# Cross-attention in a decoder kernel: the plain scores of two heads issued ahead of the two turned ones in each step

## The reference: what is computed

```python
# b = 32 slices of 128 rows, 8 heads of 16 rows; q is the normalised x, k and v are the context
qh = q.reshape(b * h, d // h, m)          # (256, 16, 256)
kh = k.reshape(b * h, d // h, -1)
vh = v.reshape(b * h, c // h, -1)
qk = einsum('bdm,bdn->bmn', qh, kh) * scale
sm = softmax(qk, axis=-1)
ret = einsum('bmn,bcn->bcm', sm, vh)
x = x + ret
```

## Time and profile before

| | us |
|---|---|
| median of 3 runs (1822.62 to 1827.89) | 1824.02 |
| the profiled execution | 1821.79 |
| its span, first to last instruction | 1819.6 |
| first to last turned score, bankXT of line 1295 | 946.6 to 1421.8 |

### The profile page before, as it was taken

How to read it: one execution, slowest core, us unless ns; L and a number is a source line. 1 busy time by engine, 2 the same in 40 slices (tenths; PEclk the granted TensorE clock), 3 DMA queues, 4 the chain that set the end, 5 groups by cost and what they waited for, 6 DMA issues and landing times. The chain is left out here.

```text
span 1819.6 us, 45303 instructions
## 1 busy us (share of the span) xinstructions
PE 1723.4 (95%) x15418; PEld 1383.0 (76%) x15419; DVE 1184.2 (65%) x2266; ACT 815.6 (45%) x1577; POOL 835.4 (46%) x1295
## 2 busy tenths in 40 slices
PE   3999999999999999999869999999999899999997
PEld 2888888888888888888757777777777799866664
DVE  5777777777777777776657788888886454422221
ACT  3434334334334334334317777777776543311111
POOL 4455555555555555555434444444443331144443
PEclk9999999999999999999869999999999899999999
DMA  5021121121121121121233444444443256422221
GB/s 187 19 60 40 48 58 38 48 58 37 49 58 36 50 58 37 49 58 39 53 98 96 119 117 117 123 119 123 124 123 97 89 159 236 136 64 68 67 63 40
DMA packets 145103, 148.17 MB, mean 81 GB/s; under 512 B 26114, under 2 KB 139718, under 8 KB 143242
## 3 DMA queue, kind: packets, MB, share of 16 engines
q1 hardware_dynamic: 138218, 120.74, 24.0%
q0 software_dynamic: 5664, 13.93, 2.4%
q10 hardware_dynamic: 1152, 12.58, 2.0%
HBM read 93.20 MB, written 53.98 MB: 81 GB/s over the span
## 5 line engine op out<-in xcount | busy, mean ns | idle before, releaser
L1195 DVE TENSOR_REDUCE xmax<-bankX 128x4 f32<-128x1024 f32 x256 | 308.7, 1217 | 63.5 <-PE bankX L1284 58.8
L1143 ACT ACTIVATE xe<-bankXT 128x512 f32<-128x512 f32 x512 | 292.0, 598 | 93.9 <-PE bankXT L1295 79.5
L1295 PE MATMUL bankXT<-stq,stk 98*128 98x256 f32 x1024 | 230.9, 312 | 11.7 <-ACT xe L1143 5.1
L369 POOL TENSOR_TENSOR roped<-ropeC,ropeD 128x512 f32<-128x512 f32 x160 | 205.2, 1289 | 56.7 <-DVE ropeD L530 56.7
L1295 PEld LDWEIGHTS bankXT<-stq,stk 98*128 98x128 f32 x1024 | 157.6, 193 | 54.7 <-ACT xe L1143 35.7
L557 DVE TENSOR_TENSOR oTl<-bankV,oTh 128x512 fp32r<-128x512 f32 x128 | 88.1, 688 | 166.7 <-ACT oTh L445 166.7
L662 PE MATMUL bankQ<-wqh,xnTh 128*128 128x512 f32 x384 | 188.9, 492 | 0.0
L1284 PE MATMUL bankX<-stk,stq 96*128 96x256 f32 x1024 | 171.1, 291 | 14.5 <-DMA rw<-in_rw 11.0
L361 POOL TENSOR_TENSOR prob<-prob,rden 128x1024 f32<-128x1024 f32 x64 | 121.9, 1904 | 88.8 <-DVE rden L553 88.4
L1284 PEld LDWEIGHTS bankX<-stk,stq 96*128 96x128 f32 x1024 | 145.0, 196 | 18.0 <-DMA rw<-in_rw 11.2
L728 PE MATMUL bankO<-woh,oTh 128*128 128x256 f32 x512 | 152.5, 298 | 0.0
(11 more groups left out here) (189 smaller groups left out, 3907.0 us busy)
## 6 DMA issues: line engine op xcount, KB each, us to landing
stackk_d<-chl SPq DMA_DIRECT2D x96, 128.0 KB, 2.3
stackq_d<-q2hl SPq DMA_DIRECT2D x96, 128.0 KB, 2.3
stk<-stackk_d SPq DMA_DIRECT2D x32, 384.0 KB
stq<-stackq_d SPq DMA_DIRECT2D x128, 96.0 KB
wexp<-in_wexp ACTq DMA_DIRECT2D x8, 1536.0 KB, 7.9
x_d<-x SPq DMA_DIRECT2D x64, 128.0 KB, 1.9
xrden<-inv_d SPq DMA_DIRECT2D x64, 128.0 KB, 2.5
xin<-xg_d SPq DMA_DIRECT2D x39, 128.5 KB, 2.1
```

The lines of the kernel that those rows point to most:

```text
L369: nc.gpsimd.tensor_tensor(roped[c % 3][:], ropeC[c % 2][:], ropeD[c % 2][:], ALU.add).then_inc(s_rsum, 1)
L1143: nc.scalar.activation(xe[q][:].rearrange("p n m -> p (n m)"), bT[:, q % 2, :], ACT.Exp).then_inc(s_xe, 1)
L1195: nc.vector.tensor_reduce(xmax[tile[1] % 2][:, :, a:b + 1:b - a].rearrange("p m h -> p h m"), bS[:, 2 * (pr % 2):2 * (pr % 2) + 2, :].rear ...
L1295: ins = nc.tensor.matmul(bT[:, q % 2, n * D:(n + 1) * D], stk[p][0:98, hd // 4, n * P:(n + 1) * P], stq[p][0:98, hd, :], start=True, stop= ...
```

## The change

In every step of PE's body in the cross-attention the plain scores of two heads are issued first, then the two turned scores. Before, the plain scores stood between the first and the second turned score. What follows at the end of a step (turns, results, logits, rank) keeps its place, and the programs of the other four engines are the same.

```diff
             def body(tile, one, two, three, four, five):
                 w, v, y = prev(tile, 1), prev(tile, 2), prev(tile, 4)
                 for r in range(STEPS):
+                    if one:
+                        scores_x(tile, r)
                     if two and r >= LAG:
                         turned_scores_x(w, 2 * (r - LAG))
                     if three and r < LAG:
                         turned_scores_x(v, 2 * (r + STEPS - LAG))
-                    if one:
-                        scores_x(tile, r)
                     if two and r >= LAG:
                         turned_scores_x(w, 2 * (r - LAG) + 1)
                     if three and r < LAG:
```

## The result

The change makes the kernel slower by 0.77%: the ratio to the kernel before is 1.0077 (95% interval 1.006 to 1.0093). The medians are 1838.6 us (5 runs, 1835.6 to 1844.3) and 1826.8 (5 runs, 1822.6 to 1829.9; three of them are those shown ahead). The forecast was 12 us more and 1836.0 as the time; the ratio says 14.1 more, and the medians are 11.8 apart. The profiled execution took 1838.6, its span 1836.5, which is 16.9 over the span before.

What follows compares the result with a forecast made beforehand. PE, 98% busy, sets the pace, with ACT chasing it through bankXT's two banks. 0.4 us a tile over 30 tiles makes 12 us more, a median of 1836.0; range 1822 to 1846 (8 in 10).

Steps and rivals of the forecast that it cites:

- The ledger: Hand-computed start times of PE's scores and ACT's exponentials through a cross-attention tile: 14.61 us before, 15.25 after, 0.64 more.
- disturbances: Some 0.2 us a tile from elsewhere before; assumed to stay in part, so 0.40 a tile was taken, not 0.64.
- The range of 5 to 19: Bounds in us on the added time: 4.5 if plain scores mostly start free, 19 if all 0.64 a tile counts; chance 0.57.
- The wait of the second turned score: Second turned score now waits for its bank, since exponentials follow 0.47 apart; waits of 0.1 to 0.25 in five steps.
- S pays the 0.10: Plain scores, first after small work or results, take 0.10 us more: 0.58 to the turned scores.
- The lower bound of the sum: Plain scores don't pay the 0.10 in five of eight places: 4.5 us more in all.
- the rival in which S is free: Plain scores first cost nothing of their own and POOL isn't late: 0 to 6 us more, centre 4, 1828; chance 0.18.
- POOL's chain: POOL's split, queued behind its scatter, holds the turned maxima in step 1: start at 7.60 in place of 7.44.
- ACT behind the results: ACT's first exponential after the results comes later than before: 0.48 us by the issue order, 0.5 as the sign.
- Filled waits: Rival: plain scores moved ahead run in PE's waits, 0.8 us a tile; half kept wins 12 us, 1812; chance 0.14.
- The load: Rival: step 0's plain scores wait for the tile's load, 0.3 us a tile, 9 us on top, 1845; chance 0.11.
- the wait for the written maxima: Step 4's first turned score waiting for maxima written to stq: can hide behind the plain scores, so fewer such waits.

Runs made afterwards that it cites:

- experiment 5: Kernel before, its order kept, with exponentials halved in the loop's tiles (results unusable, only timed): ratio 0.9968 to the kernel before.
- experiment 6: Kernel before with the new order and exponentials halved in the loop's tiles (results unusable, only timed): ratio 0.9976 to the kernel before.
- experiment 7: Kernel before, its order kept, exponentials halved in the loop's tiles and the load issued 1.4 us earlier (only timed): ratio 0.9945 to the kernel before.
- experiment 8: Kernel before with the new order, exponentials halved in the loop's tiles and the load issued 1.4 us earlier (only timed): ratio 0.9924 to the kernel before.
- experiment 1: Kernel before with plain scores first only in steps 2 and 6, right behind the results: ratio 1.0111 to the kernel before, 20 us more.
- experiment 3: Kernel before with both turned scores first and plain scores last in all steps: ratio 1.0089 to the kernel before, 16 us more.
- experiment 11: New order, with POOL splitting the maxima ahead of its scatter: ratio 1.0068 to the kernel before, 12 us more.
- experiment 10: New order, with SP issuing the next tile's load at the start of its body, about 8 us earlier: ratio 1.0081 to the kernel before.
- experiment 2: Kernel before with plain scores first in steps 0, 1, 3, 4, 5 and 7 only: ratio 1.0054 to the kernel before, 10 us more.
- experiment 4: Kernel before with plain scores first in steps 0, 1, 7, last in 2, 4, 6, unchanged in 3, 5: ratio 1.0051, 9 us more.
- experiment 12: Kernel before with plain scores first in step 1, last in 2, 4, 6, unchanged elsewhere, and the load 1.4 us earlier: ratio 0.9997 to the kernel before.
- experiment 9: Kernel before, its order kept, with SP issuing the next tile's load at the start of its body, about 8 us earlier: ratio 1.0002.

## Why the prediction was right

**The order of the tile.** The ledger gave 15.25 a tile. S of step 0 stands at 1118.97, 1134.33 and 1149.66 in the profile after, 15.36 and 15.33 apart. The ledger of before gave 14.61 where the earlier trace rows have 14.66. So the difference of the two ledgers, 0.64, has its match in 0.68 of undisturbed tiles. The means are harder. From the end of body 4 to the end of body 31 lie 27 tile lengths, 400.8 us before (995.26 to 1396.06) and 415.1 after (995.19 to 1410.29), 0.53 a tile. The forecast took 0.40, because it let the longer tile swallow 0.24 of disturbances. It swallowed little: over 16 tiles in the middle of the loop the means are 14.81 (1070.51 to 1307.48) and 15.41 (1072.53 to 1319.04), 0.60 apart. What brings the 0.60 down to 0.53 are the last tiles, behind the loop, where undisturbed ones are only some 0.45 apart (1381.40 to 1396.06 before, 1395.19 to 1410.29 after); why, is open. So the mechanism was right, the credit for disturbances too large, and that 12 came so near to 14 is in part luck. The range of 5 to 19 didn't need it.

```profile
1118.97 0.72 PE L1284 MATMUL bankX<-stk,stq 96*128 96x256 f32 x4
```

```profile
1134.33 0.73 PE L1284 MATMUL bankX<-stk,stq 96*128 96x256 f32 x4
```

```profile
1149.66 0.72 PE L1284 MATMUL bankX<-stk,stq 96*128 96x256 f32 x4
```

**The wait of the second turned score.** It opened as forecast, no longer than 0.3, some six times a tile. That the cost comes from the time that ACT takes for a head is shown by the halved exponentials (experiments 5 to 8): the 14 us fall to between 1.5 and minus 3. They shorten the distance of two exponentials and the time until a bank is free together, so they don't tell the one from the other; that it is the distance is argued from the neighbouring turned scores (experiments 1 and 3).

**S pays the 0.10, or most of it.** Behind results and small work it takes 0.58, 0.55 and 0.56 to the turned scores (1108.46 to 1109.04, 1109.66 to 1110.21, 1100.74 to 1101.30), against 0.48 in a stream (1105.24 to 1105.72). The lower bound of the sum, and with it the rival in which S is free, is out. So is what the weight loads' rule (the Trainium skill, TensorE: Matmul & The Clock Gate, Step-by-step: what each phase is for), by which a later load is pulled ahead of matmuls in flight, would make of this place: the measurement decides. The weight loads in the profile after, behind the results of step 1, show it:

```profile
1108.46 0.53 PEld L1284 LDWEIGHTS bankX<-stk,stq 96*128 96x128 f32 x4 [0.41 <-issue]
1108.92 0.55 PEld L1295 LDWEIGHTS bankXT<-stq,stk 98*128 98x128 f32 x4
```

S's first load starts at 1108.46, together with its matmul; that of the turned score behind it starts 0.12 ahead of its own (1109.04). Behind small work, at 1109.66, the load is only 0.03 ahead (1109.63).

**POOL's chain.** The turned maxima waited for it 17 times, 4.0 us in 23 tiles, 0.17 a tile; the ledger had 0.16. That it is charged in full was right for the undisturbed tile: experiment 11 gave back 0.19 there.

**ACT behind the results.** 0.47 later behind `nd` and 0.48 behind `sh`, as forecast. Experiment 3 costs as much without it. Whether it costs anything by itself no run tells, since S ahead of the first turned score always makes the turned scores neighbours.

**The rivals.** Filled waits: no, PE waits more often, not less. The load: not in the full change (experiment 10), though its waits came up in versions with a shorter tile (experiments 2, 4, 5 and 6).

**What was missing.** One tile in four is longer than the others, in both kernels. In the kernel after, S of step 0 starts there 0.48 behind the turn ahead of it (1103.21 to 1103.69 above) in place of 0.14 (1118.83 to 1118.97), and again four tiles on, at 1164.86 to 1165.34. The loop's body is four tiles long, and the gap lies where it begins, so its jump back is the likely reason, but no run isolates it. From turn to turn such a tile takes 15.62 (1103.21 to 1118.83). The kernel before has it too, 14.94 against 14.67:

```profile
1099.85 0.39 PE L1274 MATMUL bankM<-const,cx 128*128 128x128 f32 x2
1114.79 0.38 PE L1274 MATMUL bankM<-const,cx 128*128 128x128 f32 x2
...
1129.90 0.39 PE L1274 MATMUL bankM<-const,cx 128*128 128x128 f32 x2
1144.57 0.39 PE L1274 MATMUL bankM<-const,cx 128*128 128x128 f32 x2
```

There the turned score of step 0 comes 0.53 or 0.54 behind the turn in every tile, so its bank wait covers the gap; the same tile loses 0.22 elsewhere, in step 4, where the turned score starts 0.64 behind logits in place of 0.42:

```profile
1107.15 0.55 PE L1335 MATMUL bankM<-rw,xn3T 128*128 128x8 f32 x4
1107.79 0.50 PE L1295 MATMUL bankXT<-stq,stk 98*128 98x256 f32 x2
```

After, S starts 0.40 or 0.41 behind logits in all tiles, and the wait for the written maxima (4.4 us in the stage before) is gone, as forecast. So the longer tile is some 0.27 over the others before and after: it is missing in both ledgers, and adds nothing to their difference.

Open: why the change costs less behind the loop than in it, what holds the turned score of step 4 before and in experiment 12, and how much of the two ends of the span is the clock alone.

## What to carry to other kernels

Where two engines pass work through two banks, the order of the producer's independent work decides: put it between the two items, so that the second item is issued when its bank comes free, since the consumer can't take two items closer together than its own pace (0.47 here, while two turned scores are 0.24 apart). Work that moves ahead of a group is free only while the group would have waited there anyway; ask what each item stood under before. A hand ledger of two engines' starts gave the added length of an undisturbed tile here (0.64 against 0.68), and promised more than came each time the tile was made shorter (experiments 4, 5, 7 and 12): then the next chains (here the reductions, a load and the write of the maxima through SP) end the waits. And where a timed ratio can't resolve a term, the length of one undisturbed tile in the trace often can (experiment 11).

## What the runs showed of the hardware

The first group of 256-column matmuls behind a result block or behind small matmuls took 0.07 to 0.10 more than the same group in a stream, whichever group it was: 0.34 against 0.24 for a turned pair, 0.55 to 0.58 against 0.48 for four plain ones. Behind the results its weight load starts together with its first matmul and not ahead of it. And in experiments 9 and 10 transfers issued some 8 us earlier (in 9 the load of `stk` 0.2 us behind the start of step 0 in place of 8.7) gained nothing: in the old order the 2.2 us of waits of the plain scores are gone, and the waits for exponentials are 5.0 longer.
